# Routing logits with the router's weights stationary: batch 0's in one group ahead of the first scores, G's copy between tile 0's halves, and batch 2's first u block split early

## The chip, the cores and the metric

The kernel runs on one NeuronCore of a Trainium2 chip. Its engines work in parallel and are ordered by semaphores: TensorE (PE; weight loads are listed apart as PEld), VectorE (DVE), ScalarE (ACT), GpSimd (POOL) and the DMA queues, which mostly SyncE (SP) feeds. The metric is the device time of one execution in microseconds, median of several; lower is better.

## The reference

Input x is 4 batches of 1024 rows of 256 floats. Everything is computed from the normalised rows:

```python
xn = layernorm(x)
q, k, v = xn @ Wq.T + bq, xn @ Wk.T + bk, xn @ Wv.T + bv
qk = q @ k.T                                     # per batch, 1024 x 1024
theta = 0.5 + 0.2 * sigmoid(qk) + 0.15 * tanh(qk) + 0.1 * relu(qk)
s = softmax(theta) @ v @ Wo.T + bo
e = argmax(xn @ Wr + br)                         # one of 8 experts per row
g = silu(gelu(xn @ W1[e] + b1[e]) @ W2[e] + b2[e])
out = x + s * g
```

## The kernel before, in words

Most products are split into three float32r matmuls: hi x hi, lo x hi, hi x lo (`product`, L899 to L901). A tile is 128 rows; there are 32 (`NT`), eight per batch (`TPB`). `M` (256 x 256, from Wq and Wk) gives u = M xn; scores are u times xn, so that q and k are never formed. `G` (from Wv and Wo) gives v. A score also needs an offset per row, `c_all` (and `c_half`, half of it), which is one more column of the router's table: `small_w` holds per row of xn 8 expert logits, the offset `E` and zeros up to 48 columns (`PAD`).

Each engine has its program written out by hand; the order in the text is the order in its queue.

- TensorE: transposes batch 0's normalised rows (`turn_0`), makes u of batch 0 (`first_u`, `u_product`), scores of tile 0, `G`, scores of tile 1 with batch 3's transposes between them (`turn`), v of batch 0, then tiles 2 to 7: `scores(n+1)`, `transposes(n)`, `values(n-1)`. Between them it turns batches 3, 2 and 1 (`TURNED`) and computes their logits (`route`). Next come the experts in sorted units of 256 rows (a half unit of 128 where an expert's count ends so), and then tiles 8 to 31 of attention. `job(n)` makes u and v of the next batches in pieces, one per tile: tile 9's and 10's are batch 2's first two blocks of u.
- `route(i, t)` takes tile t of `kept` (transposed rows, fp32) as the stationary operand and streams `small_w` (48 columns) through it, into bank 7; `logits_done` counts batches. `route_0(t)` does that for batch 0 out of `xnT_hi` and `xnT_lo` with `R_parts` (hi and lo of the table) into bank 6: tiles 0 to 3 behind the u products, tiles 4 to 7 between G's four matmuls, with two counts of `logits_done` and of `c_ready`.
- ScalarE: high parts (`high_u`, `high_v`, ...), three activations per half of a tile (`acts`), exponentials (`exps`), gelu; `square_root` for the normalisation.
- VectorE: low parts, `row_statistics`, `variances`, `scales`, the combination of the three activations (`thetas`), `take_turned` (logits and offsets out of bank 7), `finish` (the tile's result out of its bank into `half_0` or `half_s`).
- GpSimd: the normalisation of batches 3, 2 and 1, each waiting for `scales_ready`, later gathers and the last products.

What `turn(i, q)` waits for sets TensorE's pace in the first 60 us: q = 0 for `xn_pool` (GpSimd's normalised rows) and for bank 7 (`G_ready`, later `logits_taken`); q = 1 for bank 6 (`c_ready` for batch 3, `half_s_ready` for batch 1).

## Time and profile before

| what | value |
|---|---|
| time, median of 3 | 527.67 us (527.51 to 527.84) |
| profiled execution's own time | 527.64 us |
| its span, first to last instruction | 525.6 us |
| busy: TensorE, VectorE, ScalarE, GpSimd | 98%, 77%, 66%, 37% |
| granted TensorE clock | 1.000 |

The span is what the trace covers; 2.0 us of the time lie around it. A busy share is an average over the whole; what an edit is worth is read in the stretch where it stands, from what ends the last wait there.

### The profile page before, as it was taken

To read this page: it belongs to the slowest core of one execution; us is meant where nothing else is said; L and a number is where in the kernel's file an instruction comes from. 1 tells how busy PE (TensorE), PEld (TensorE's weight loads), DVE (VectorE), ACT (ScalarE), POOL (GpSimd) and SP (SyncE) were. 2 spreads that over 40 slices of the span, in tenths; PEclk is the share of its full clock that TensorE was granted. 3 is DMA by queue.
4 is the path that set the end of the run, shared out by engine and by line. 5 is a ranking of instruction groups with operands and counts; after the bars stand their busy time and mean duration, and the time that the engine had idled before them with its cause. 6 is when DMAs were issued, how large, how long until landed. Compare 5 with 4: busy or idle time off the path is not lost.

```text
span 525.6 us, 10829 instructions
## 1 busy us (share of the span) xinstructions
PE 515.6 (98%) x3773; PEld 484.3 (92%) x3773; DVE 402.6 (77%) x811; ACT 344.6 (66%) x633; POOL 195.8 (37%) x227
## 2 busy tenths in 40 slices
PE   7999999999999999999999989999999999999997
PEld 6899998899989999899999979998999989999997
DVE  5898689946578855598555688768999998867887
ACT  4789778437356733466343575899787786777884
POOL 3218419913112222222112222005676785342441
PEclk9999999999999999999999999999999999999999
DMA  8964720031635711247311421005233232211221
GB/s 266 344 225 176 285 81 1 2 120 32 230 123 151 255 55 41 61 133 237 112 40 40 136 70 42 21 22 190 62 99 113 71 114 87 62 44 49 60 71 51
DMA packets 40754, 57.49 MB, mean 109 GB/s; under 512 B 3654, under 2 KB 35788, under 8 KB 40156
## 3 DMA queue, kind: packets, MB, share of 16 engines
q1 hardware_dynamic: 35452, 46.02, 26.5%
q0 software_dynamic: 3488, 9.47, 6.4%
q10 hardware_dynamic: 1760, 1.32, 0.8%
q8 instruction: 28, 0.46, 0.4%
q14 instruction: 26, 0.21, 0.1%
HBM read 41.07 MB, written 17.56 MB: 112 GB/s over the span
## 4 chain that ended last, share of the span: by engine, by line
PE 86%; ACT 6%; DVE 5%; issue 1%; POOL 1%; DMA 1%; ACTq 0%; DVEq 0%
PE ps L899 26%; PE ps L901 25%; PE ps L900 25%; PE ps L1014 5%; DVE stats L1375 2%; PE ps L1193 1%; PE ps L1080 1%; ACT hid L763 1%; POOL xn_all L464 1%; DMA xn_all<-in_L_attn_x_dram 1%; PE ps L1070 1%; ACT relu_s L628 1%; ACT tanh_s L625 1%; ACT theta L624 1%; PE ps L1045 1%
## 5 line engine op out<-in xcount | busy, mean ns | idle before, releaser
L899 PE MATMUL ps<-v_hi,pT_hi 128*128 128x258 f32 x256 | 74.9, 293 | 0.2
L747 ACT ACTIVATE hid<-ps,b_now 128x256 f32<-128x256 f32 x128 | 53.7, 472 | 29.7 <-PE ps L901 28.8
L900 PE MATMUL ps<-v_lo,pT_hi 128*128 128x258 f32 x256 | 72.5, 283 | 0.0
L901 PE MATMUL ps<-v_hi,pT_lo 128*128 128x258 f32 x256 | 72.3, 282 | 0.0
L1430 DVE SCALAR_TENSOR_TENSOR theta<-tanh_s,theta 128x512 f32<-128x512 f32 x64 | 47.3, 739 | 23.5 <-ACT tanh_s L625 22.9
L899 PE MATMUL ps<-w_hi_even,hidT_h 128*128 128x256 f32 x200 | 58.5, 293 | 1.6 <-DVE hidT_l L1727 1.1
L636 ACT ACTIVATE theta<-theta,neg_max 128x512 f32<-128x512 f32 x64 | 43.0, 720 | 24.9 <-DVE neg_max L1436 24.6
L519 POOL COPY unit_token<-sorted_token 128x2 int32 x19 | 4.5, 238 | 142.9 <-PE ps L1193 142.9
L901 PE MATMUL ps<-w_hi_even,hidT_l 128*128 128x256 f32 x200 | 56.6, 283 | 0.0
L900 PE MATMUL ps<-w_lo_even,hidT_h 128*128 128x256 f32 x200 | 56.6, 283 | 0.0
L778 ACT ACTIVATE g_sb<-y_sb 128x512 f32<-128x512 f32 x20 | 12.6, 631 | 65.8 <-DVE y_sb L1742 65.8
L624 ACT ACTIVATE theta<-ps,c_half 128x512 f32<-128x512 f32 x64 | 44.3, 692 | 17.4 <-PE ps L901 17.3
L510 POOL DMA_INDIRECT row<-xn_rows,unit_token x38 | 44.1, 1161 | 20.7 <-POOL unit_token L519 14.9
L899 PE MATMUL ps<-xnT_hi,u_hi 128*128 128x512 f32 x128 | 51.7, 404 | 0.0
L526 POOL DMA_INDIRECT g_tile<-sorted_g,slot_g x32 | 37.5, 1171 | 38.0 <-DMA sorted_g<-g_sb 32.7
L901 PE MATMUL ps<-xnT_hi,u_lo 128*128 128x512 f32 x128 | 50.4, 394 | 0.0
L900 PE MATMUL ps<-xnT_lo,u_hi 128*128 128x512 f32 x128 | 50.0, 391 | 0.0
L899 PEld LDWEIGHTS ps<-v_hi,pT_hi 128*128 128x128 f32 x256 | 48.4, 189 | 1.7 <-issue 1.2
L901 PE MATMUL ps<-rowT_h,w_lo_even 128*128 128x256 f32 x176 | 49.8, 283 | 0.0
L899 PE MATMUL ps<-rowT_h,w_hi_even 128*128 128x256 f32 x176 | 49.8, 283 | 0.0
L900 PE MATMUL ps<-rowT_l,w_hi_even 128*128 128x256 f32 x176 | 49.8, 283 | 0.0
L900 PEld LDWEIGHTS ps<-v_lo,pT_hi 128*128 128x128 f32 x256 | 48.6, 190 | 0.3
(258 smaller groups left out, 1641.5 us busy)
## 6 DMA issues: line engine op xcount, KB each, us to landing
w_raw_odd<-in_L_ffn_W_dram SPq DMA_DIRECT2D x10, 1024.0 KB
w_raw_even<-in_L_ffn_W_dram SPq DMA_DIRECT2D x6, 1024.0 KB
sorted_g<-g_sb SPq DMA_DIRECT2D x20, 256.0 KB, 2.2
xn_rows<-xn_all SPq DMA_DIRECT2D x4, 1024.0 KB, 6.2
x_tile<-in_L_attn_x_dram SPq DMA_DIRECT2D x32, 128.0 KB, 2.2
out_dram<-g_tile SPq DMA_DIRECT2D x32, 128.0 KB, 1.7
xn_all<-in_L_attn_x_dram SPq DMA_DIRECT2D x3, 1024.0 KB, 12.4
kept_xT<-passing_xT SPq DMA_DIRECT2D x2, 1024.0 KB, 4.0
```

Of the source, the lines that this page charges most:

```text
L510: pool.indirect_dma_start(row[:, a, :], None, xn_rows, bass.IndirectOffsetOnAxis(ap=tokens[:, a:a + 1], axis=0)).then_inc(row_in, 16)
L526: pool.indirect_dma_start(g_tile[:, p % RING, :], None, sorted_g, bass.IndirectOffsetOnAxis(ap=slot_g[:, n:n + 1], axis=0)).then_inc(g_in[ ...
L624: nc.scalar.activation(theta[:, j % 2, cols], bank, ACT.Tanh, bias=c_half[:, n:n + 1], scale=0.5)
L636: nc.scalar.activation(part, part, ACT.Exp, bias=neg_max[:, j % 2, 1:2], scale=-1.0, accum_out=exp_sums[:, h:h + 1] if n == NT - 1 else No ...
L747: last = nc.scalar.activation(hid[:, j % 2, c * UNIT:(c + 1) * UNIT], ps[:, HID_BANK + j, c * UNIT:(c + 1) * UNIT], ACT.Gelu, bias=b1_now[ ...
L778: nc.scalar.activation(g_sb[:, :, :], y_sb[:, :, :], ACT.Tanh, scale=0.5).then_inc(y_tanh, 1)
L899: mm(dst, a_hi, b_hi, start=first, stop=False)
L900: mm(dst, a_hi, b_lo, start=False, stop=False)
L901: return mm(dst, a_lo, b_hi, start=False, stop=last)
L1014: last = nc.tensor.transpose(pT_bank(n, h)[:, i * P:(i + 1) * P], theta[:, n % 2, h * HALF + i * P:h * HALF + (i + 1) * P], ident[:, :])
L1375: last = v.bn_stats(stats[:, i, :], xn_all[:, i, :])
L1430: v.scalar_tensor_tensor(part, tanh_s[:, cols], KT, part, ALU.mult, ALU.add).then_inc(mixed, 1)
```

## The change

- Router's table stationary. For the group g of 0 to 3, `spread_w` (batches 3, 2, 1) and `R_parts` (batch 0) hold the table's columns at column 32 g of a 128 x 128 operand, zeros elsewhere; the rows that stream through it are those of 32-row group g of all eight tiles, 256 columns in 8 runs of 32. The four groups and two halves of the contraction add up in one 128 x 256 result, and a 32 x 32 block transpose on VectorE brings it into `logits_t`, rows on partitions.
- Batch 0's logits are one block of 16 such matmuls between the u products and tile 0's scores, one count of `logits_done` and `c_ready` for all eight tiles. The other batches' blocks stand whole behind v's last piece and behind `values`.
- ScalarE copies `G_hi` between tile 0's two halves of activations; VectorE puts two tiles of statistics ahead of tile 0's first half and two behind it.
- ScalarE normalises one tile of batch 0 instead of two, VectorE two instead of one, and VectorE's copy of the biases stands ahead of the second statistics.
- In an expert's first unit, `Else` in place of a second `If` (ScalarE, VectorE).
- Batch 2's first block of u is split (`high_u`, `low_u`) at the last expert unit instead of behind tile 10's exponentials; at tile 10 TensorE makes the second block ahead of the tile's transposes.

```diff
+    SPREAD = P + 32
...
-        R_parts = sb("R_parts", [P, DC, PAD], F32R)
+        with ExitStack() as first_routing:
+            R_parts = view(first_routing, "R_parts", [P, DC, 4 * SPREAD], F32R)
...
+        with ExitStack() as routing:
+            spread_w = view(routing, "spread_w", [P, DC, 4 * P])
...
             act.wait_ge(scales_ready, 1)
-            normalize(range(2))
+            normalize(range(1))
...
+            act.wait_ge(key_kept, 1)
+            for g in range(4):
+                nc.scalar.activation(spread_w[:, :, g * SPREAD:g * SPREAD + SM], small_w[:, :, 0:SM], ACT.Copy
+                                     ).then_inc(spread_ready, 1)
             for q in range(2, 4):
                 high_u(0, q)
...
             act.wait_ge(c_ready, 1)
-            for h in range(2):
-                acts(0, h)
+            acts(0, 0)
             act.wait_ge(G_done, 1)
             nc.scalar.activation(G_hi[:, :, :], pair_of(ps[:, 7, :]), ACT.Copy).then_inc(G_high, 1)
+            acts(0, 1)
...
-                with act.If(full < u0 + 1):
+                with act.Else():
...
+            def first_job():
+                high_u(*next_job(TPB + 1)[1:])
+
             with act.If(last_u < full_7):
                 gelus(last_u, 1)
+                first_job()
             with act.If(full_7 < last_u + 1):
-                gelus_half(last_u, 1)
+                gelus_half(last_u, 1, beside=first_job)
...
-                    if job:
+                    if job and n > TPB + 1:
                         (high_u if job[0] == "u" else high_v)(*job[1:])
-                if routed_batch is not None and q % 2:
-                    for t in range(2 * q - 2, 2 * q + 2):
-                        route(routed_batch, t)
+                if routed_batch is not None and q == 3:
+                    route(routed_batch)
...
-                    if routed_batch is not None and i % 4 == 3:
-                        for t in range(i - 3, i + 1):
-                            route(routed_batch, t)
+                    if routed_batch is not None and i == TPB - 1:
+                        route(routed_batch)
...
                     if i == 0:
-                        pe.wait_ge(c_ready, 2)
+                        pe.wait_ge(c_ready, 1)
...
+            def group_of(rows, g):
+
+                return rows.rearrange("p (i g j) -> p g i j", g=4, j=32)[:, g]
+
+            def route(i):
 
                 kept = passing_xT if i < 2 else own_xT
...
+                pe.wait_ge(turned_kept, 4 * i + 4)
+                pe.wait_ge(spread_ready, 4)
+                for g in range(4):
+                    for k in range(DC):
+                        last = mm(ps[:, 7, 0:TPB * 32], spread_w[:, k, g * P:(g + 1) * P], group_of(kept[:, k, :], g),
+                                  start=g == 0 and k == 0, stop=g == 3 and k == DC - 1)
+                last.then_inc(logits_done, 1)
+
+            def route_0():
+
+                pe.wait_ge(R_ready, 1)
+                for g in range(4):
+                    for k in range(DC):
+                        mm(ps[:, 6, 0:TPB * 32], R_parts[:, k, g * P:(g + 1) * P], group_of(xnT_hi[0][:, k, :], g),
+                           start=g == 0 and k == 0, stop=False)
+                        last = mm(ps[:, 6, 0:TPB * 32], R_parts[:, k, g * P:(g + 1) * P], group_of(xnT_lo[0][:, k, :], g),
+                                  start=False, stop=g == 3 and k == DC - 1)
+                last.then_inc(logits_done, 1)
...
-            u_product(0, 2, [0, 1])
-            u_product(0, 3, [2, 3])
+            u_product(0, 2)
+            u_product(0, 3)
+            route_0()
             pe.wait_ge(u_ready, 2)
             scores(0)
...
-                    if m == DC - 1 and ec == DC - 1:
-                        last.then_inc(G_done, 1)
-                    route_0(4 + 2 * m + ec)
+            last.then_inc(G_done, 1)
...
+                elif n == TPB + 2:
+                    job(n)
+                    pe.wait_ge(pT_ready, n * 2)
+                    transposes(n)
+                    weighted(n - 1)
                 else:
+            v.memset(spread_w[:, :, :], 0.0)
+            v.memset(R_parts[:, :, :].bitcast(F32), 0.0)
...
-            normalize(range(2, 3))
-            dve.wait_ge(x0_in[1], 16)
-            statistics = row_statistics(range(4, TPB))
+            normalize(range(1, 3))
             dve.wait_ge(biasT_done, 1)
             v.tensor_copy(bias_cols[:, :], ps[:, 6, BIAS_COL:BIAS_COL + 3 * DC]).then_inc(bias_kept, 1)
-            step(statistics)
+            dve.wait_ge(x0_in[1], 16)
+            step(row_statistics(range(4, TPB)))
...
+            tiles = slice(0, TPB)
             dve.wait_ge(logits_done, 1)
-            score_offsets_0(slice(0, 4))
+            step(v.transpose(logits_t[:, :, :].rearrange("p i n -> p (i n)"), ps[:, 6, 0:TPB * 32]))
+            step(v.tensor_scalar(c_all[:, tiles], logits_t[:, :, E], kappa[:, 0:1], None, ALU.add))
+            step(v.tensor_tensor(c_all[:, tiles], logits_t[:, :, SM + E], c_all[:, tiles], ALU.add))
+            v.tensor_scalar(c_half[:, tiles], c_all[:, tiles], 0.5, None, ALU.mult).then_inc(c_ready, 1)
             scales(2, 3 * TPB, 4 * TPB)
...
             def take_turned(i):
                 b = TURNED[i]
-                dve.wait_ge(logits_done, 3 + i)
+                dve.wait_ge(logits_done, 2 + i)
                 now = slice(b * TPB, (b + 1) * TPB)
-                source = padded(ps[:, 7, 0:TPB * PAD])
-                take_logits(now, source)
-                score_offsets(i, now, source[:, :, E])
-
-            thetas(0, [0])
+                v.transpose(logits_t[:, :, :].rearrange("p i n -> p (i n)"), ps[:, 7, 0:TPB * 32]).then_inc(logits_taken, 1)
+                dve.wait_ge(logits_taken, i + 1)
+                score_offsets(now, logits_t[:, :, E])
+                take_logits(now, logits_t)
...
             dve.wait_ge(x_in[2], 16)
             row_statistics(range(2 * TPB, 2 * TPB + 2))
+            thetas(0, [0])
+            row_statistics(range(2 * TPB + 2, 2 * TPB + 4))
...
-            dve.wait_ge(logits_done, 2)
-            take_logits(slice(0, TPB), logits_0)
+            take_logits(slice(0, TPB), logits_t)
...
-                with dve.If(full < u0 + 1):
+                with dve.Else():
...
-                if next_job(n):
+                if next_job(n) and n > TPB + 1:
...
+            low_u(*next_job(TPB + 1)[1:])
             thetas(TPB + 1)
```

How rows move. The rows below are instructions in program order: line, operation, output <- inputs, output shape; xN is a run. Lines of the change are some 10 higher than those of before (L899 to L901 are L912 to L914).

TensorE of before, batch 0 from u's third block on (`M` is the moving side's partner, `R_parts` the table):

```order
L1111 MATMUL ps<-ident,wo_raw 128x128 x4
L899 MATMUL ps<-xnT_hi,M_hi 128x512
L900 MATMUL ps<-xnT_lo,M_hi 128x512
L901 MATMUL ps<-xnT_hi,M_lo 128x512
L1094 MATMUL ps<-R_parts,xnT_hi 128x48
L1096 MATMUL ps<-R_parts,xnT_lo 128x48
L1094 MATMUL ps<-R_parts,xnT_hi 128x48
L1096 MATMUL ps<-R_parts,xnT_lo 128x48
L899 MATMUL ps<-xnT_hi,M_hi 128x512
```

And of the change, from the end of u's fourth block to tile 0's scores, with the last rows of the block and, behind four products, G:

```order
L914 MATMUL ps<-xnT_hi,M_lo 128x512
L1103 MATMUL ps<-xnT_hi,R_parts 128x256
L1105 MATMUL ps<-xnT_lo,R_parts 128x256
...
L1103 MATMUL ps<-xnT_hi,R_parts 128x256
L1105 MATMUL ps<-xnT_lo,R_parts 128x256
L912 MATMUL ps<-xnT_hi,u_hi 128x512
...
L1132 MATMUL ps<-woT,wv_raw 128x256 x4
L1136 MATMUL ps<-woT,bv_wide 128x256 x2
```

Eight groups of four small matmuls, four between u's products and four between G's, have become one block of 16 wide ones; G's matmuls stand together.

VectorE of before, from the statistics of batch 3 to tile 0's first half:

```order
L1375 BN_STATS stats<-xn_all 128x6 x8
L1382 BN_AGGR mean_var<-stats 128x2 x8
L1384 TENSOR_SCALAR std<-mean_var 128x8
L1533 TENSOR_SCALAR c_all<-ps,kappa 128x4
L1534 TENSOR_TENSOR c_all<-ps,c_all 128x4
L1535 TENSOR_SCALAR c_half<-c_all 128x4
L1389 RECIPROCAL rstd<-std 128x8
L1390 SCALAR_TENSOR_TENSOR shift<-mean_var,rstd 128x8
L1410 SCALAR_TENSOR_TENSOR u_lo<-ps,r_col,u_hi 128x512 x2
L1430 SCALAR_TENSOR_TENSOR theta<-tanh_s,theta 128x512
```

And of the change:

```order
L1396 TENSOR_SCALAR std<-mean_var 128x8
L1545 STREAM_TRANSPOSE logits_t<-ps 128x256
L1546 TENSOR_SCALAR c_all<-logits_t,kappa 128x8
L1547 TENSOR_TENSOR c_all<-logits_t,c_all 128x8
L1548 TENSOR_SCALAR c_half<-c_all 128x8
L1401 RECIPROCAL rstd<-std 128x8
L1402 SCALAR_TENSOR_TENSOR shift<-mean_var,rstd 128x8
L1422 SCALAR_TENSOR_TENSOR u_lo<-ps,r_col,u_hi 128x512 x2
L1387 BN_STATS stats<-xn_all 128x6 x2
L1441 SCALAR_TENSOR_TENSOR theta<-tanh_s,theta 128x512
```

The transpose now stands between `std` and `shift`, and `shift` is what GpSimd's normalisation of batch 3 waits for.

TensorE of before at tile 10 (end of tile 11's scores, tile 10's transposes, u's block, tile 9's values):

```order
L901 MATMUL ps<-xnT_hi,u_lo 128x512
L1014 MATMUL ps<-ident,theta 128x128 x8
L899 MATMUL ps<-xnT_hi,M_hi 128x512
L900 MATMUL ps<-xnT_lo,M_hi 128x512
L901 MATMUL ps<-xnT_hi,M_lo 128x512
...
L899 MATMUL ps<-v_hi,pT_hi 128x258
```

And of the change:

```order
L914 MATMUL ps<-xnT_hi,u_lo 128x512
L912 MATMUL ps<-xnT_hi,M_hi 128x512
L913 MATMUL ps<-xnT_lo,M_hi 128x512
L914 MATMUL ps<-xnT_hi,M_lo 128x512
L912 MATMUL ps<-xnT_hi,M_hi 128x512
L913 MATMUL ps<-xnT_lo,M_hi 128x512
L914 MATMUL ps<-xnT_hi,M_lo 128x512
L1024 MATMUL ps<-ident,theta 128x128 x8
L912 MATMUL ps<-v_hi,pT_hi 128x258
```

u's block has moved from behind the transposes to ahead of them.

## Rows read from the trace of the kernel before

**Rows 1.** The cores' spans and granted TensorE clock; then the page's first part.
```profile
core 0: 525.6 us, clock 1.000
...
PE 515.6 (98%) x3773; PEld 484.3 (92%) x3773; DVE 402.6 (77%) x811; ACT 344.6 (66%) x633; POOL 195.8 (37%) x227
```

**Rows 2.** Timeline of TensorE, 16 to 32 us (start us, us, instruction).
```profile
16.65 0.18 PE L1094 MATMUL ps<-R_parts,xnT_hi 128*128 128x48 f32 x1
...
17.01 0.48 PE L899 MATMUL ps<-xnT_hi,M_hi 128*128 128x512 f32 x1
...
23.30 0.60 PE L1123 MATMUL ps<-woT,wv_raw 128*128 128x256 f32 x2
...
27.49 0.58 PE L899 MATMUL ps<-xnT_hi,u_hi 128*128 128x512 f32 x1
...
28.37 1.39 PE L1070 MATMUL ps<-ident,xn_all 128*128 128x128 f32 x8
...
31.00 1.04 PE L1070 MATMUL ps<-ident,xn_all 128*128 128x128 f32 x8
```

**Rows 3.** What TensorE waited for (us in total, times, longest).
```profile
PE ps L899 <- DVE hidT_l L1727: 1.1, 1, 1.1
...
PE ps L926 <- ACT xn_all L568: 0.3, 1, 0.3
```

**Rows 4.** Timeline of TensorE and ScalarE, 342 to 370 us.
```profile
342.65 1.67 ACT L763 ACTIVATE hid<-ps,b_now 128x128 f32<-128x128 f32 x6 [0.75 <-PE ps L1248]
...
357.98 0.39 PE L899 MATMUL ps<-xnT_hi,u_hi 128*128 128x512 f32 x1
...
359.11 1.09 PE L1014 MATMUL ps<-ident,theta 128*128 128x128 f32 x8 [0.29 <-DVE pT_lo L1451]
...
362.13 0.28 PE L899 MATMUL ps<-v_hi,pT_hi 128*128 128x258 f32 x1
...
367.76 1.03 PE L1014 MATMUL ps<-ident,theta 128*128 128x128 f32 x8
...
370.02 0.28 PE L899 MATMUL ps<-v_hi,pT_hi 128*128 128x258 f32 x1
```

**Rows 5.** Chain of waits at 50 us; timeline of TensorE at 71 us.
```profile
50.15 1.72 PE ps L1080 x16
...
71.15 0.28 PE L1153 MATMUL ps<-running,ones_r 128*128 128x256 f32 x1
71.27 0.17 PE L1154 MATMUL ps<-running,ones_r 128*128 128x8 f32 x1
```

**Rows 6.** Timelines of VectorE, GpSimd, ScalarE and TensorE in the first 12 us.
```profile
1.16 0.28 DVE L1478 MEMSET keep_scan<- 128x264 f32 x1
...
5.33 1.41 DVE L1375 BATCH_NORM_STATS2 stats<-xn_all 128x6 f32<-128x256 f32 x4 [3.60 <-DMA xn_all<-in_L_attn_x_dram]
...
8.03 0.41 DVE L1484 TENSOR_SCALAR xn_all<-xn_all,rstd,shift 128x256 f32<-128x256 f32 x1
...
10.29 0.75 DVE L1490 TENSOR_TENSOR M_lo<-ps,M_hi 128x256 fp32r<-128x256 f32 x2
...
8.11 0.69 POOL L464 TENSOR_SCALAR xn_all<-xn_all,rstd,shift 128x256 f32<-128x256 f32 x1 [3.93 <-DVE shift L1390]
...
10.52 0.58 ACT L657 ACTIVATE xnT_hi<-ps 128x512 fp32r<-128x512 f32 x1
...
10.92 1.17 PE L947 MATMUL ps<-xnT_hi,M_hi 128*128 128x512 f32 x4
```

**Rows 7.** Timeline of GpSimd, 22 to 49 us.
```profile
22.35 5.20 POOL L464 TENSOR_SCALAR xn_all<-xn_all,rstd,shift 128x256 f32<-128x256 f32 x8 [9.83 <-DVE shift L1390]
...
38.60 10.44 POOL L464 TENSOR_SCALAR xn_all<-xn_all,rstd,shift 128x256 f32<-128x256 f32 x16 [10.67 <-DVE shift L1390]
```

**Rows 8.** Timeline of VectorE at 56 us.
```profile
56.06 0.48 DVE L1465 SCALAR_TENSOR_TENSOR half<-ps,rden,attn_const 128x256 f32<-128x256 f32 x1
```

**Rows 9.** Chain of waits at 307 us; ACTq is ScalarE's queue.
```profile
306.93 0.04 ACTq L804
```

More of the change, by code:

```diff
@@ L708, in _ @@
                 high_v(0, q)
-            act.wait_ge(c_ready, 2)
             for n in range(1, TPB):
@@ L839, in tile_8 @@
             def tile_8():
-                act.wait_ge(c_ready, 5)
+                act.wait_ge(c_ready, 4)
                 act.wait_ge(w1_split, 2 * E - 2)
@@ L979, in u_product @@
                         last.then_inc(u_done, 1)
-                    for t in routed[k:k + 1]:
-                        route_0(t)
             def v_product(b, q, routed_batch=None):
@@ L1416, in low_v, with score_offsets @@
                                 v_hi[place_of_batch(b)][:, 2 * q:2 * q + 2, 0:D].bitcast(F32), ALU.subtract).then_inc(v_ready, 1)
-            def score_offsets(i, cols, source):
-                v.tensor_scalar(c_all[:, cols], source, kappa[:, 0:1], None, ALU.add).then_inc(logits_taken, 1)
-                dve.wait_ge(logits_taken, i + 1)
+            def score_offsets(cols, source):
+                step(v.tensor_scalar(c_all[:, cols], source, kappa[:, 0:1], None, ALU.add))
                 v.tensor_scalar(c_half[:, cols], c_all[:, cols], 0.5, None, ALU.mult).then_inc(c_ready, 1)
@@ L1586, in _ @@
                                    ).then_inc(const_kept, 1)
-            row_statistics(range(2 * TPB + 2, 3 * TPB))
+            row_statistics(range(2 * TPB + 4, 3 * TPB))
             dve.wait_ge(x_in[1], 16)
@@ L1760, in first_unit_of @@
                     low_w1(e, other, 0)
-                with dve.If(full < u + 1):
+                with dve.Else():
                     parts_half(u, beside=lambda: low_w1(e, other, 0))
```

45 lines of the change are left out of this document (9 added, 36 removed).

## The prediction

> **What bounds the kernel now.** I read the profile's page and the granted clock first: TensorE is busy 515.6 us of 525.6 us at full clock (1.000 throughout, its 2.4 GHz level), VectorE 77%, ScalarE 66% [rows 1]. So a microsecond taken from TensorE counts only if no wait takes its place, and a stall of TensorE elsewhere is worth as much as work. Then the list of what TensorE waited for, and its timeline around the edits: from 16 to 30 us it runs without a gap [rows 2], the longest waits behind the start are 1.1 us on `hidT_l` and 0.3 us on ScalarE's rows [rows 3], and a stall stands at 359 us [rows 4]. Last the timelines of VectorE and GpSimd beside it: they say when `xn_all`, `G_lo` and `c_all` are ready if TensorE comes earlier. The profiled execution took 527.64 us, the median is 527.67, so I sum against 527.64 and need no correction.
>
> **Batch 0's routing on TensorE.** Before: 32 matmuls of 48 columns. Four of them take 0.36 us from the first to the next product (16.65 to 17.01), and that product's first matmul then runs some 0.09 us slower, so 0.45 us per four, 3.6 us in all [rows 2]. After: 16 of 256 columns. The same kind of instruction (float32r, 256 columns in 8 runs of 32 elements) stands at L1153: the next starts 0.12 us behind it [rows 5]. 16 x 0.12 = 1.9 us. TensorE's own work falls by 1.7 us, 0 to 0.2 us less if the runs cost anything.
>
> **The other three batches' routing.** Before, 16 trace records (8 matmuls) take 1.72 us, 32 of them 3.44 us per batch, and 0.1 us for switching [rows 5]. After, 8 full fp32 matmuls of 256 columns. G's and the constant's are of that size: six of them and 16 small ones take 27.49 - 23.30 = 4.19 us, less 4 x 0.45 is 2.39, so 0.40 each; with the slower matmul behind them 0.44 [rows 2]. 8 x 0.435 = 3.5 us. I book 0, with 0.3 us either way over the two batches where TensorE sets the pace.
>
> **The start.** TensorE waits 0.3 us for ScalarE's two tiles [rows 3]. With one tile on ScalarE and two on VectorE (8.03 + 0.41, some 0.33 more) the last of the four is GpSimd's, 8.11 + 0.69 = 8.80 [rows 6]. That alone gains 0.3 us. But the second tile and the bias copy (which now stands ahead of the statistics) push VectorE's statistics, and with them the square root that stands in ScalarE's queue ahead of the second `xnT_hi` (10.52), by about 0.33 + 0.22 = 0.55 us. That copy would end at 10.52 + 0.58 + 0.55 = 11.65, and the third of the four matmuls of 10.92 needs it at 10.92 + 0.32 + 0.23 = 11.47 [rows 6]. So the 0.3 us turns into a loss of 0.2 to 0.3; I take +0.27 for everything behind it. The two memsets (1024 and 1280 elements; 264 take 0.28, so 1.0 and 1.3 us) fit into the 3.6 us in which VectorE waits for x [rows 6]. The four small copies of `spread_w` stand in ScalarE's idle time before u's third block.
>
> One thing could make the start worse: VectorE's second tile held until GpSimd's ends at 8.80, 0.35 us that the whole chain below would take over. GpSimd's tile beside VectorE's took 0.69 us, against 5.20 / 8 = 0.65 in the long run of them [rows 6, 7], so nothing was held before and I book nothing. The Trainium skill speaks for the hold: its page SBUF — State Buffer, section Who interferes with whom, says that a VectorE tensor_scalar in a two-port mode and GpSimd exclude each other for a whole instruction. By that rule the sum would end 0.35 us higher; this trace, with 0.69 us, doesn't bear it out.
>
> **Where batch 0's 1.7 us go.** TensorE would arrive at batch 3's transposes (28.37 before [rows 2]) at 28.37 - 1.7 + 0.27 = 26.95. They need `xn_all` of batch 3: GpSimd's eight tiles, 22.35 + 5.20 = 27.55 [rows 7]. Those wait for VectorE's `shift`, and ahead of that the change puts the 128x256 transpose out of PSUM. No row has it. Bounds: 0.28 us (a memset of 264 elements, no source at all) and 0.75 us (two `M_lo` operations, 512 elements from PSUM); nearest is one of them, 256 elements, 0.75 / 2 = 0.375 us [rows 6]; I take 0.42 with its wait. So GpSimd ends at 27.55 + 0.27 + 0.42 = 28.24 and TensorE starts there at about 28.3, not at 26.95. `G_lo` is ready before that, about 27.9, although G now waits for one half of tile 0's activations only. Of 1.7 us 1.4 become a new wait on GpSimd. What is gained: the second transpose group no longer waits for `c_ready` 2; these eight took 1.39 us from the first's start to the last's end, the next eight, at 31.00, 1.04 [rows 2]. So TensorE leaves 0.35 + 0.07 = 0.4 us earlier.
>
> **On to batch 2 and 1.** The next group waits for GpSimd's batch 2 (38.60 + 10.44 / 2 = 43.8 [rows 7]). That hangs on tile 1's activations, which follow tile 0's: VectorE's two c_all steps less and two statistics tiles moved ahead bring theta of tile 0 about 0.55 us forward, so 0.6 us here. Batch 1's second group needs `half_0` of tile 0, since it writes the bank that tile's result lies in. Before, it started at 56.6, some 1.7 us behind the routing's end: VectorE did logits, c_all, c_half, then `half` (56.06 + 0.48) [rows 8]. Now all 8 routing matmuls stand at the end and the transpose comes first: 0.42 + 0.2 + 0.2 + 0.3 + 0.2 + 0.5 + 0.1 = 1.9 to 2.0 us. 0.3 us of the 0.6 are lost again. **Front: 0.3 us gained**, between -0.3 (transpose 0.75, VectorE's tile held until 8.80) and +0.7.
>
> **The experts.** `Else` instead of a second `If` drops one compare on ScalarE and VectorE. The only half unit that opens an expert is at 307 us, where TensorE's wait of 1.1 us [rows 3] hangs on ScalarE's queue, in which the compare and its operand's computation stand (0.04 us each, with gaps as long) [rows 9]. 0.1 us.
>
> **Around 359 us.** Tile 11's scores end their last slots 0.69 us (three matmuls of 0.23) behind 357.98, at 358.67; tile 10's transposes start at 359.11, 0.44 late, held by `pT_lo`. From them to the values it takes 362.13 - 359.11 = 3.02 us, for tile 11 370.02 - 367.76 = 2.26 with the same work: 0.76 us more, in which u's product waits for `u_lo` [rows 4]. After: batch 2's first u block is split some 17 us earlier, in a gap in which ScalarE waited 0.75 us for TensorE [rows 4] and VectorE waited too, and the second block's product (six matmuls, 1.4 us) stands ahead of the transposes and covers the 0.44. 0.44 + 0.76 = 1.2 us are gained, 1.15 with something for the early copy. What ScalarE and VectorE no longer do at 359 keeps them ahead of TensorE for the tiles behind; I count half a microsecond of margin left at tile 11's transposes. If ScalarE's early copy (the one of 0.58 us is its like [rows 6]) does not fit the gap whole, it delays tile 9's activations by 0.1. **1.15 us**, 0.5 to 1.3.
>
> **Sum.** 527.64 - 0.3 - 0.1 - 1.15 = 526.1, and the median's 0.03 us more change nothing in it.
>
> **Rivals.**
> - Batch 0's saving arrives in full, because the transposes are not held by GpSimd (the start does not slip, the stall at batch 1 does not grow): 527.64 - 1.7 - 0.1 - 1.15 = 524.7. Against it: GpSimd's 5.2 us start no earlier in any reading.
> - The front gives nothing or costs 0.3 (a transpose of 0.75, or VectorE's second tile held by GpSimd's: 0.35 us turn +0.3 into about 0): 526.4 to 526.8. For it: each step of the front hangs on VectorE's queue.
> - The stall at 359 only moves: the margin of 0.5 us at tile 11 is used up and returns as a wait on `pT_lo`. 527.64 - 0.3 - 0.1 - 0.2 = 527.0.
> - Slower: the fp32 routing matmuls read their 8 runs badly. Sixteen of them stand where TensorE sets the pace; at 0.435 + 1.55 / 16 = 0.53 us each the gain is gone, at 0.60 the kernel is slower by 0.2%, at twice the price 16 x 0.435 = 7.0 us give 533. Against it: L1153 reads such runs at full rate [rows 5], though in the other number format.
>
> **How the numbers follow.** 0.2% (1.06 us, so below 526.6) is about what a measurement can tell here. Forecast (525.5 to 526.5): 0.58; full saving: 0.10; empty front: 0.20, a third of it below 526.6; stall moved: 0.08; slow matmuls: 0.04. Faster 0.58 + 0.10 + 0.07 = 0.75, same 0.20, slower 0.05 (0.04 and what nobody listed). The range 525.0 to 526.9 leaves out most of the full saving, half of the moved stall and the slow matmuls.
>
> **What would show it.** TensorE waits over 1 us on GpSimd's `xn_all` at about 27 us and starts the transposes at 28.2 to 28.4; a transpose of 0.35 to 0.5 us ahead of `shift`; routing blocks of 3.5 us per batch; a wait of 0.6 us on `half` near 56 us; no waits on `pT_lo` and `u_lo` at 359. Wrong if the transposes start near 27, if the start slips by more than 0.5 us, or if a stall stands at tile 11 or 12.

## The result, and the profile after

The changed kernel took 526.48 us (median of 9, 525.39 to 527.29), the kernel before in the same comparison 527.57 us (median of 9, 527.30 to 528.18). The ratio is 0.9977 (95% interval 0.9969 to 0.9986): 1.1 us faster. The predicted time was 526.1 us. Two things beside the medians matter below: the changed kernel's times are spread over 1.9 us and those of the kernel before over 0.9, and the total came out near the forecast although two of its parts did not: the front lost where a gain was booked, and a gain that nobody booked made up for it.

The profiled execution of the changed kernel took 526.14 us with a span of 523.8. This is the page's first part, to be held against [rows 1]:

```profile
core 0: 523.8 us, clock 1.000
...
PE 512.4 (98%) x3709; PEld 480.1 (92%) x3709; DVE 407.2 (78%) x814; ACT 344.7 (66%) x636; POOL 194.4 (37%) x227
```

TensorE has 64 instructions and 3.2 us of busy time less, and yet the span fell by only 1.8 us, because waits came in. They stand in the list of what TensorE waited for (us in total, times, longest), which answers to [rows 3]:

```profile
PE ps L1079 <- POOL xn_all L470: 1.3, 1, 1.3
PE ps L912 <- DVE hidT_l L1737: 1.1, 1, 1.1
PE ps L1079 <- DVE half L1476: 0.8, 1, 0.8
PE ps L939 <- DVE xn_all L1496: 0.7, 1, 0.7
PE ps L1255 <- ACT hid L766: 0.3, 1, 0.3
PE ps L960 <- ACT xnT_hi L663: 0.2, 1, 0.2
```

The first and the third are the waits that the prediction named. The waits on `pT_lo` and `u_lo` at 359 us are gone. The fourth and the last are at the start. A `...` in a view marks rows left out.

TensorE's timeline of the changed kernel shows the front and the stretch at 359 us; it answers to [rows 2] and [rows 4]:

```profile
11.73 0.73 PE L960 MATMUL ps<-xnT_hi,M_hi 128*128 128x512 f32 x2 [0.25 <-ACT xnT_hi L663]
...
16.23 0.48 PE L912 MATMUL ps<-xnT_hi,M_hi 128*128 128x512 f32 x1
...
19.07 0.28 PE L1103 MATMUL ps<-xnT_hi,R_parts 128*128 128x256 f32 x1
...
20.98 0.40 PE L912 MATMUL ps<-xnT_hi,u_hi 128*128 128x512 f32 x1
...
28.48 1.09 PE L1079 MATMUL ps<-ident,xn_all 128*128 128x128 f32 x8 [1.27 <-POOL xn_all L470]
...
39.28 3.61 PE L1094 MATMUL ps<-passing_xT,spread_w 128*128 128x256 f32 x16
42.55 0.58 PE L912 MATMUL ps<-xnT_hi,u_hi 128*128 128x512 f32 x1
...
56.96 0.66 PE L1079 MATMUL ps<-ident,xn_all 128*128 128x128 f32 x4 [0.76 <-DVE half L1476]
...
360.09 1.03 PE L1024 MATMUL ps<-ident,theta 128*128 128x128 f32 x8
...
366.64 1.03 PE L1024 MATMUL ps<-ident,theta 128*128 128x128 f32 x8
```

The same point of the program, by its start in either trace, tells how far the changed kernel is ahead or behind. It is 0.37 us behind at the u product at 16.23 (before: 15.86), 0.11 behind at batch 3's transposes (28.48 against 28.37; most expectations call them tile 3's), 0.13 ahead at 43.7, 0.37 behind at 60, 0.3 behind at 100, 0.16 behind at 298, 0.03 ahead at 308, level at 348, 1.12 ahead at tile 11's transposes (366.64 against 367.76), still 1.1 at 391, and 1.87 ahead at 517. So the gain is made of 0.2 at 308, 1.1 at 359, and two pieces that come in small steps where no instruction was changed: 0.2 between 60 and 298 and 0.75 between 399 and 517. The front loses.

On VectorE, the timeline of the changed kernel, which answers to [rows 6] and [rows 8]:

```profile
2.72 1.12 DVE L1491 MEMSET R_parts<- 128x1280 f32 x1 [0.21 <-issue]
...
8.05 0.91 DVE L1496 TENSOR_SCALAR xn_all<-xn_all,rstd,shift 128x256 f32<-128x256 f32 x2
8.88 0.14 DVE L1512 COPY bias_cols<-ps 128x6 f32<-128x6 f32 x1
8.95 1.39 DVE L1387 BATCH_NORM_STATS2 stats<-xn_all 128x6 f32<-128x256 f32 x4
...
21.70 0.44 DVE L1545 STREAM_TRANSPOSE logits_t<-ps 128x256 f32<-128x256 f32 x1
...
27.51 0.67 DVE L1586 TENSOR_TENSOR G_lo<-ps,G_hi 128x512 fp32r<-128x512 f32 x1
28.10 0.44 DVE L1559 TENSOR_TENSOR logits<-logits_t,br_all 128x64 f32<-128x64 f32 x1
28.57 0.35 DVE L1589 TENSOR_TENSOR logits<-logits,logits_t 128x64 f32<-128x64 f32 x1
28.95 0.69 DVE L1441 SCALAR_TENSOR_TENSOR theta<-tanh_s,theta 128x512 f32<-128x512 f32 x1
...
37.91 0.25 DVE L1401 RECIPROCAL rstd<-std 128x16 f32<-128x16 f32 x1 [0.46 <-ACT std L570]
...
55.46 0.35 DVE L1432 TENSOR_SCALAR c_all<-logits_t,kappa 128x8 f32<-128x8 f32 x1
...
55.92 0.26 DVE L1559 TENSOR_TENSOR logits<-logits_t,br_all 128x64 f32<-128x64 f32 x1
...
56.42 0.48 DVE L1476 SCALAR_TENSOR_TENSOR half<-ps,rden,attn_const 128x256 f32<-128x256 f32 x1
```

Three VectorE rows of before, for the same stretch:

```profile
24.37 0.70 DVE L1430 SCALAR_TENSOR_TENSOR theta<-tanh_s,theta 128x512 f32<-128x512 f32 x1 [0.80 <-ACT tanh_s L625]
...
27.21 0.69 DVE L1574 TENSOR_TENSOR G_lo<-ps,G_hi 128x512 fp32r<-128x512 f32 x1 [0.50 <-ACT G_hi L692]
...
28.97 0.69 DVE L1430 SCALAR_TENSOR_TENSOR theta<-tanh_s,theta 128x512 f32<-128x512 f32 x1
```

And GpSimd of the changed kernel, against [rows 7]:

```profile
23.23 5.20 POOL L470 TENSOR_SCALAR xn_all<-xn_all,rstd,shift 128x256 f32<-128x256 f32 x8 [10.13 <-DVE shift L1402]
```

### The profile page after: what moved, and what is told of

The parts are those of the page before. It is cut to its first block, busy times and chain, and to the rows that moved or that the text cites. A ratio compares the mean times of both kernels' runs of the same rounds, so it can differ in the third digit from the quotient of the medians.

```text
span 523.8 us, 10703 instructions
## 1 busy us (share of the span) xinstructions
PE 512.4 (98%) x3709; PEld 480.1 (92%) x3709; DVE 407.2 (78%) x814; ACT 344.7 (66%) x636; POOL 194.4 (37%) x227
## 4 chain that ended last, share of the span: by engine, by line
PE 89%; DVE 5%; ACT 3%; POOL 1%; issue 1%; DMA 1%; ACTq 0%; DVEq 0%
PE ps L912 27%; PE ps L914 26%; PE ps L913 26%; PE ps L1024 5%; PE ps L1200 1%; PE ps L1094 1%; DVE stats L1387 1%; POOL xn_all L470 1%; DMA xn_all<-in_L_attn_x_dram 1%; ACT hid L772 1%; PE ps L1079 1%; PE ps L1054 1%; DVE u_lo L1422 1%; PE ps L1255 0%; PE ps L960 0%
## 5 line engine op out<-in xcount | busy, mean ns | idle before, releaser
L912 PE MATMUL ps<-v_hi,pT_hi 128*128 128x258 f32 x256 | 74.8, 292 | 0.1
L914 PE MATMUL ps<-v_hi,pT_lo 128*128 128x258 f32 x256 | 72.2, 282 | 0.0
L1441 DVE SCALAR_TENSOR_TENSOR theta<-tanh_s,theta 128x512 f32<-128x512 f32 x64 | 48.4, 756 | 20.1 <-ACT tanh_s L631 19.4
L912 PE MATMUL ps<-w_hi_even,hidT_h 128*128 128x256 f32 x200 | 58.6, 293 | 1.6 <-DVE hidT_l L1737 1.1
L914 PE MATMUL ps<-w_hi_even,hidT_l 128*128 128x256 f32 x200 | 56.5, 283 | 0.0
L912 PE MATMUL ps<-xnT_hi,u_hi 128*128 128x512 f32 x128 | 51.8, 405 | 0.0
L914 PE MATMUL ps<-xnT_hi,u_lo 128*128 128x512 f32 x128 | 50.2, 392 | 0.0
L912 PEld LDWEIGHTS ps<-v_hi,pT_hi 128*128 128x128 f32 x256 | 48.3, 189 | 1.7 <-issue 1.1
L912 PE MATMUL ps<-rowT_h,w_hi_even 128*128 128x256 f32 x176 | 49.8, 283 | 0.0
L914 PE MATMUL ps<-rowT_h,w_lo_even 128*128 128x256 f32 x176 | 49.8, 283 | 0.0
```

The costliest lines, as they stand in the source:

```text
L912: mm(dst, a_hi, b_hi, start=first, stop=False)
L914: return mm(dst, a_lo, b_hi, start=False, stop=last)
L1441: v.scalar_tensor_tensor(part, tanh_s[:, cols], KT, part, ALU.mult, ALU.add).then_inc(mixed, 1)
```

## Experiments

Each kernel was timed beside the kernel before on the same chip; the kernels of one group shared those runs. The kernel before had medians of 527.41, 527.54 and 527.46 us in the three groups. finish_between, start_before, all_three, start_finish and four are medians of 5 executions, the others of 8 to 11.

### First group: the tail, the front, the wait on `half`, the wait on GpSimd

**tail_only**: the kernel before with the edit around 359 us alone.

```diff
+            def first_job():
+                high_u(*next_job(TPB + 1)[1:])
...
+            low_u(*next_job(TPB + 1)[1:])
             thetas(TPB + 1)
...
+                elif n == TPB + 2:
+                    job(n)
+                    pe.wait_ge(pT_ready, n * 2)
+                    transposes(n)
+                    weighted(n - 1)
```

> The kernel before with only the last item of the change: batch 2's first u block split at the last expert unit, and its second block ahead of tile 10's transposes. Theory (the whole gain is the stall at 359 us): 1.1 to 1.2 us faster than before, ratio about 0.9978, and in the trace no wait on pT_lo or u_lo near 359, transposes of tile 11 and later 1.1 us earlier. Rival (the stall only moves, or the gain of the changed kernel comes from the front and from the late tiles' pace): under 0.5 us, ratio 0.999 or more.

Measured: 526.24 us (526.09 to 527.33), ratio 0.9980 (0.9971 to 0.9990), 1.2 us faster. Its trace is 0.16 us behind that of before at 348 us and 0.98 ahead at 375: a gain of 1.14, inside the 1.1 to 1.2 expected. The tail is worth what was booked, without the front.

**front_only**: the changed kernel without the tail's edit and with the second `If` again.

> The changed kernel without its tail edits and with the second If restored: only the first 70 us are changed. Theory (batch 0's saving of 1.7 us becomes a wait on GpSimd, and the block transposes delay the rest): 0.2 to 0.4 us slower than before, ratio 1.0004 to 1.0008, TensorE reaches tile 3's transposes 0.2 to 0.4 us later than before. Rival (the front gains, as the prediction had it): 0.3 us faster, ratio 0.9994.

Measured: 526.99 us (526.54 to 527.79), ratio 0.9992 (0.9983 to 1.0001). By the median that is a gain of 0.4 us and nearer to the rival, but the interval holds 1, so the medians decide nothing. The trace says more. It is of one of the longer executions (527.74 us), 1.04 us behind that of before at batch 3's transposes and 1.07 at 348 us, so up to there the front only costs. Then, from 399 us on, it catches up 0.76 us in the last stage, as the changed kernel did and as tail_only did not. Its first 13 us show where the lag comes from. First VectorE, then TensorE:

```profile
9.84 0.17 DVE L1503 COPY bias_cols<-ps 128x6 f32<-128x6 f32 x1 [1.03 <-PE ps L924]
9.93 1.40 DVE L1378 BATCH_NORM_STATS2 stats<-xn_all 128x6 f32<-128x256 f32 x4
```

```profile
6.50 3.16 PE L919 MATMUL ps<-wk_raw,wq_raw 128*128 128x256 f32 x8
9.59 0.22 PE L924 MATMUL ps<-ident,bias_rows 6*128 6x6 f32 x1
...
17.20 0.48 PE L908 MATMUL ps<-xnT_hi,M_hi 128*128 128x512 f32 x1
```

**finish_between**: the changed kernel, with the reciprocal and `half` of tile 0 between batch 2's transposition and its offsets.

```diff
                 dve.wait_ge(logits_taken, i + 1)
+                if between:
+                    between()
                 score_offsets(now, logits_t[:, :, E])
...
-            take_turned(1)
-            finish(0)
+            take_turned(1, lambda: finish(0))
```

> The changed kernel with tile 0's result (rden and half, 0.65 us) taken on VectorE right behind batch 2's block transpose, ahead of the offsets and the logits. Theory (the 0.76 us wait on half near 56 us is VectorE's order alone): the wait falls to 0.2 or nothing, 0.5 to 0.7 us faster than the changed kernel, so 525.8 to 526.0 us. Rival (another wait stands right behind it, on the turned rows or the exponentials): the wait on half goes and TensorE reaches tile 3's transposes no earlier.

Measured: 525.27 us (524.90 to 525.91), ratio 0.9963 (0.9949 to 0.9977). Its TensorE timeline has the eight transposes in one piece, without the wait:

```profile
55.52 1.29 PE L1079 MATMUL ps<-ident,xn_all 128*128 128x128 f32 x8
```

From there on it is 0.8 us ahead of the changed kernel (0.43 ahead of before at 60 us, where the changed kernel was 0.37 behind). The stall at 56 us was worth 0.8 us by the traces. The median fell by 1.2, more than the 0.5 to 0.7 expected; against padded, a changed kernel of the same group, it is 1.0 lower. No trace shows the rest, and the changed kernel's times alone spread over 1.9 us.

**padded**: the changed kernel with nine needless 256-column matmuls ahead of tile 1's scores.

> The changed kernel with nine needless float32r matmuls of 256 columns (9 x 0.12 = 1.1 us) on TensorE ahead of tile 1's scores. Theory (TensorE waits 1.27 us there for GpSimd's rows): no change of time, the wait on xn_all falls from 1.27 to about 0.2 us. Rival (TensorE's work sets the pace there): 1.1 us slower.

Measured: 526.31 us (525.37 to 526.93), ratio 0.9976 (0.9965 to 0.9986). TensorE's timeline:

```profile
26.84 1.42 PE L1140 MATMUL ps<-M_hi,xnT_hi 128*128 128x256 f32 x9
...
29.12 1.09 PE L1079 MATMUL ps<-ident,xn_all 128*128 128x128 f32 x8 [0.17 <-POOL xn_all L470]
```

The wait on GpSimd went from 1.3 to 0.2 us and the time stayed: 1.1 us of batch 0's saving on TensorE can be spent on nothing and is not missed. This execution, too, had a late start (u product at 16.90), which is why the transposes stand at 29.12.

### Second group: the start, the lie of the tiles, GpSimd's begin

**start_before**: the changed kernel with its first 10 us as before.

```diff
-            normalize(range(1))
+            normalize(range(2))
...
-            normalize(range(1, 3))
+            normalize(range(2, 3))
+            dve.wait_ge(x0_in[1], 16)
+            statistics = row_statistics(range(4, TPB))
             dve.wait_ge(biasT_done, 1)
             v.tensor_copy(bias_cols[:, :], ps[:, 6, BIAS_COL:BIAS_COL + 3 * DC]).then_inc(bias_kept, 1)
-            dve.wait_ge(x0_in[1], 16)
-            step(row_statistics(range(4, TPB)))
+            step(statistics)
```

> The changed kernel with only its start put back: ScalarE normalises tiles 0 and 1, VectorE tile 2, and the copy of the bias columns stands behind the second half's statistics again. In the four profiles at hand whose VectorE copies the bias columns ahead of those statistics, the first u product of batch 0 starts at 16.2, 16.2, 16.9 and 17.2 us, and the bias transposition that the copy waits for ends at 8.4, 8.6, 9.5 and 9.8; in the two profiles with the old order it starts at 15.9 and 16.0, although there the transposition ended at 8.8 and 9.3. Theory (the copy's place passes every late start of TensorE on to the whole front): the u product at 15.8 to 16.1, GpSimd's last normalisation begins near 22.9 and TensorE's transposes of tile 3 near 28.1, the lowest and the highest time are within 1 us of each other (changed kernel: 1.9 us), and the median is 525.7 to 526.0 (changed kernel: 526.48). Rival (the spread and the slip have another cause, the bigger memsets or the group of routing matmuls): u product again at 16.2 or later and a median of 526.3 to 526.6.

Measured: 525.38 us (525.18 to 525.55), ratio 0.9961 (0.9947 to 0.9974). That is 1.1 us less than the changed kernel and more than was expected, and the spread fell from 1.9 to 0.4 us. The bigger memsets and the routing block are still in it, so the rival fell. The edit puts back the tiles of both engines and the place of the copy together; their shares were not tried apart. Its TensorE timeline:

```profile
6.20 1.90 PE L923 MATMUL ps<-wk_raw,wq_raw 128*128 128x256 f32 x8
8.02 0.22 PE L928 MATMUL ps<-ident,bias_rows 6*128 6x6 f32 x1
...
15.83 0.48 PE L912 MATMUL ps<-xnT_hi,M_hi 128*128 128x512 f32 x1
```

Over all traces of this study the pattern holds. With the new start, a bias transposition at 8.14, 8.30, 8.40, 9.22, 9.28 and 9.59 us gave a u product at 16.23, 16.27, 16.18, 16.85, 16.90 and 17.20. With the old one, 8.02, 8.09, 8.40, 8.59, 8.60, 8.64, 9.08 and 9.11 gave 15.83, 15.84, 15.85, 16.01, 15.86, 15.98, 15.91 and 15.95. So the new start costs 0.35 us at best and 1.3 when TensorE's first products are late, and the old one hides the lateness. The spans of all executions say the same, less sharply: they vary by 1.1 to 1.8 us within each of the six kernels with the new start and by 0.3 to 1.1 within those with the old one.

**moved**: the kernel before with one allocation moved and no instruction touched.

```diff
         G_hi, G_lo = sb("G_hi", [P, DC, D], F32R), sb("G_lo", [P, DC, D], F32R)
-        R_parts = sb("R_parts", [P, DC, PAD], F32R)
         small_w = sb("small_w", [P, DC, PAD])
...
         slot_f = sb("slot_f", [P, NT])
+        R_parts = sb("R_parts", [P, DC, PAD], F32R)
```

> The kernel before with one line moved: the 384 bytes per partition of R_parts are allocated behind slot_f and no longer ahead of small_w, so that all tiles between lie 384 bytes lower, as they do in the changed kernel. No instruction is added, removed or moved. In the last stage (399 to 479 us) a tile takes 7.97 us on TensorE in the profiles of the kernel before and of the tail alone, and 7.91 in the four profiles that hold the front edit; over the stage and the six tiles behind it that is 0.6 to 0.8 us. Theory A (where the tiles lie sets that pace): 7.91 us a tile and a median of 526.6 to 526.9. Theory B (something else of the front edit sets it, or chance): 7.97 us a tile and a median of 527.2 to 527.6.

Measured: 526.66 us (526.27 to 527.84), ratio 0.9982 (0.9973 to 0.9991): 0.9 us faster with the same program. Theory A. Two tiles of the last stage, tile starts on TensorE, ten tiles apart; first the kernel before, then this one:

```profile
431.19 1.04 PE L1014 MATMUL ps<-ident,theta 128*128 128x128 f32 x8
...
505.23 1.04 PE L1014 MATMUL ps<-ident,theta 128*128 128x128 f32 x8
```

```profile
430.99 1.03 PE L1014 MATMUL ps<-ident,theta 128*128 128x128 f32 x8
...
504.49 1.04 PE L1014 MATMUL ps<-ident,theta 128*128 128x128 f32 x8
```

74.04 us became 73.50. At 298 us the moved kernel is 0.18 ahead, at 517 us 0.82. In the last tiles, which hold no product of u or v, the scores take 2.74 us a tile instead of 2.77 and the products of `v` and `pT` 2.97 instead of 2.99, while the eight transposes take 0.79 in both. Earlier in the stage the products that make u and v, 1.50 us a tile, do not change either. So what the old place costs sits in the scores and in the products of `v` and `pT`.

**scales_first**: the changed kernel with batch 3's scales ahead of the transposition.

> The changed kernel with batch 3's scales and shifts (0.4 us) ahead of the transposition of batch 0's logits and no longer behind the offsets. GpSimd's eight normalisations, which began at 23.2 us, then begin at 22.3 to 22.5 and end at 27.5 to 27.7, with TensorE at its transposes of tile 3 by 27.3. Theory (TensorE's wait of 1.3 us is that late begin): the wait falls to 0.2 to 0.5 us and the median to 525.5 to 525.9. Rival (theta of tile 0, 0.92 us twice on VectorE, is the next to be late): the wait falls but TensorE waits for theta or pT of tile 0 near 31.5, and the median is 526.1 to 526.4.

Measured: 526.17 us (525.46 to 527.20), ratio 0.9973 (0.9964 to 0.9982), 0.3 us below the changed kernel and within its spread. My theory fell; the median lies in the rival's range, but TensorE waited neither for theta nor for `pT`. The wait did not shrink, it changed its name. In the list of TensorE's waits:

```profile
PE ps L1079 <- DVE G_lo L1586: 1.5, 1, 1.5
```

The transposes write the bank in which G lies, and VectorE must have computed `G_lo` from it first. In the changed kernel's trace `G_lo` ended at 28.18 and GpSimd at 28.43 us: both conditions were met within 0.3 us of each other, and taking one away shows the other.

**all_three**: start_before, finish_between and scales_first together.

> The changed kernel with the start of the kernel before, with batch 3's scales ahead of the transposition, and with the first steps of batch 0's finish between batch 2's transposition and its offsets. If the three gains add (0.5, 0.8 and 1.0 us by the two expectations beside this one and by the measured 525.27 for the third), the median is 524.2 to 524.6. If scales first and the start hide each other (both move GpSimd's begin, and TensorE then has no more wait there), it is 524.6 to 525.0.

Measured: 524.72 us (524.57 to 525.34), ratio 0.9953 (0.9939 to 0.9966), above the sum of three gains and in the second range: scales first added nothing.

### Third group: the lie of the tiles again, and the best version

**moved_back**: the changed kernel with 384 unused bytes ahead of `small_w`.

```diff
+        unused = sb("unused", [P, DC, PAD], F32R)
         small_w = sb("small_w", [P, DC, PAD])
```

> The changed kernel with 384 bytes per partition that nothing uses allocated ahead of small_w, so that small_w and the tiles behind it up to slot_f lie again where they lie in the kernel before. No instruction is changed. If where the tiles lie is worth the 0.9 us that the kernel before gained by the move, this kernel loses as much: tiles at 7.97 us in the last stage and a median of 527.1 to 527.5, level with the kernel before. If the changed kernel does not react to it: 7.91 us a tile and a median of 526.3 to 526.7.

Measured: 526.66 us (525.68 to 527.57), ratio 0.9985 (0.9976 to 0.9994). The expected loss of 0.7 us does not show in the median, which is 0.2 above that of the changed kernel; both have the spread of the late start, so the medians can't decide. The traces do. The changed kernel's two tiles, then this one's:

```profile
429.94 1.03 PE L1024 MATMUL ps<-ident,theta 128*128 128x128 f32 x8
...
503.45 1.03 PE L1024 MATMUL ps<-ident,theta 128*128 128x128 f32 x8
```

```profile
430.47 1.04 PE L1025 MATMUL ps<-ident,theta 128*128 128x128 f32 x8
...
504.51 1.04 PE L1025 MATMUL ps<-ident,theta 128*128 128x128 f32 x8
```

73.51 us became 74.04, the kernel before's figure to the hundredth. The place of the tiles costs this trace what was expected; the median shows a loss of 0.2 us (0.4 by the ratios, whose intervals overlap) of the 0.7 expected, and that gap stays open.

**moved_half**: the kernel before with the tiles 192 bytes lower instead of 384.

> The kernel before with its tiles 192 bytes lower instead of 384 (R_parts moved as before, and 192 unused bytes in its place). If the pace falls in step with the distance, or depends on lying at a multiple of 384, the median is between the two, 526.9 to 527.2, or that of the kernel before; if a shift of 192 does what one of 384 does, it is 526.5 to 526.8. I know no reason for one above the other.

Measured: 526.63 us (526.30 to 527.14), ratio 0.9984 (0.9975 to 0.9993), the gain of the full shift. Its two tiles:

```profile
431.08 1.04 PE L1015 MATMUL ps<-ident,theta 128*128 128x128 f32 x8
...
504.48 1.04 PE L1015 MATMUL ps<-ident,theta 128*128 128x128 f32 x8
```

73.40 us. The distance is not what counts; the old place was a bad one among three.

**start_finish**: start_before and finish_between together.

> The changed kernel with the start of the kernel before and with the first steps of batch 0's finish between batch 2's transposition and its offsets, without scales first. The start alone gave 525.38 us; the wait for half is 0.8 us in its profile. Theory (the two gains are apart in time and add): 524.5 to 524.7, with no wait for half near 56 us; then the batch 3 scales of the kernel with all three (524.72) gave nothing. Rival: 524.9 to 525.4.

Measured: 524.63 us (524.38 to 525.57), ratio 0.9945 (0.9931 to 0.9958), the lowest median of the study, 1.9 us below the changed one and 2.8 below the kernel before. It has no wait on `half`, and all_three is level with it, so batch 3's scales gave nothing.

**four**: all_three with `G_lo` two statistics earlier.

```diff
-            row_statistics(range(2 * TPB + 2, 2 * TPB + 4))
             dve.wait_ge(G_high, 1)
             v.tensor_tensor(G_lo[:, :, :], pair_of(ps[:, 7, :]), G_hi[:, :, :].bitcast(F32), ALU.subtract
                             ).then_inc(G_ready, 1)
+            row_statistics(range(2 * TPB + 2, 2 * TPB + 4))
```

> The kernel with all three edits, and G_lo's subtraction on VectorE ahead of the two row statistics (0.7 us) that stood before it. In that kernel TensorE's transposes of tile 3 waited 1.5 us and began at 28.3, right behind G_lo's end (28.2), while GpSimd had been done since 27.35. Theory (with GpSimd early, G_lo is what the transposes wait for): they begin at 27.5 to 27.7, the wait is 0.7 to 0.9 us, and the median is 523.9 to 524.2. Rival (theta of tile 0 on VectorE is as late as ever and takes the gain back at tile 0's transposes near 31.5): TensorE waits there and the median is 524.5 to 524.8.

Measured: 524.96 us (524.61 to 525.13), ratio 0.9951 (0.9938 to 0.9965), above both ranges. The transposes started at 27.84, 0.5 us earlier than in all_three, with a wait of 0.85. Eight microseconds later the gain was lost. In its TensorE timeline:

```profile
27.84 1.06 PE L1079 MATMUL ps<-ident,xn_all 128*128 128x128 f32 x8 [0.85 <-DVE G_lo L1588]
...
36.22 0.39 PE L912 MATMUL ps<-G_hi,xnT_hi 128*128 128x256 f32 x1 [0.63 <-ACT relu_s L634]
```

The rival was right in kind and wrong in place: not theta near 31.5 on VectorE, but v's product at 36.2, which waits until ScalarE's `relu_s` has read its scores. VectorE's theta of tile 0's second half came no earlier than in all_three (28.87 against 28.69, after a start 0.17 later), as the rival had it, and ScalarE's exponentials and tile 1's activations follow it. After GpSimd and VectorE, ScalarE is the third engine that holds this stretch.

## Why the prediction came out right, step by step

The total was within 0.4 us of the measured one, and the sign was right. Two terms of it were not, and they cancelled: that the sum came out is luck. The clock that it read as 1.000 throughout was at its lower level for the first 5.8 to 9.1 us, which differs from one execution to the next, and the change made the front wait for it.

- **Around 359 us, 1.15 us gained:** right. 1.14 in the trace of tail_only, 1.12 in that of the changed kernel (0.00 at 348 us, 1.12 ahead at 366.64), and no stall at tile 11 or 12.
- **The experts, 0.1 us gained:** right in mechanism, 0.19 in the trace (0.16 behind at 298 us, 0.03 ahead at 308; front_only, which keeps the second `If`, gains nothing there). Up to that point front_only differs from the changed kernel in the second `If` alone, so the 0.19 us are `Else`'s; the rest of the change was not needed for it (start_before and finish_between gain 0.19 there too).
- **Batch 0's routing:** right. The sixteen matmuls took 0.12 us each (19.07 to 20.98, 1.91 us). TensorE arrived at 27.2, waited 1.27 us for GpSimd and began at 28.48 (booked 28.3), and padded shows that 1.1 of the 1.7 us are unused. The transposition took 0.44 us (booked 0.42). The 0.4 us by which TensorE was to leave earlier were 0.2 (29.33 against 29.52).
- **The other batches' routing, 0:** the block in fp32 took 3.27 us from its first matmul to the next product (39.28 to 42.55), plus 0.1 us for the slower matmul behind it, 0.1 less than the 3.5 worked out.
- **Front, "0.3 us gained": this step failed.** It lost 0.37 us in the profiled execution (at 60 us) and 1.0 to 1.2 us in those of padded, scales_first and front_only. Three parts of it were mis-sized. First, the start: booked 0.27 us, measured 0.3 to 1.3 at the u product, and over the 0.5 us that the prediction named as a sign of being wrong in three of the six traces. The working counted for VectorE's copy only the time that it takes, 0.22 us, as if TensorE's bias transposition always were done by then. The copy is a wait on TensorE, and its place ahead of the statistics puts the whole chain of the front behind an event that moves by 1.6 us between executions (8.02 to 9.59 us), with the moment at which the clock rises. Second, the 0.6 us forward for tile 1: theta of tile 0's second half began at 28.95, where it had begun at 28.97. Before, VectorE had waited 0.80 us for ScalarE ahead of the first theta and 0.50 ahead of `G_lo`; now it has no idle time from 23 to 31 us, begins that stretch later, and three of its operations beside GpSimd took longer (0.92 for 0.70 at the first theta, 0.44 and 0.35 for 0.27 and 0.28 at the logits, one input of which now lies in SBUF and no longer in PSUM). VectorE's own steps for tile 1 did come forward by the booked amount, its theta to 36.03 from 36.70, but it then waited 0.46 us for ScalarE's square root, which stands behind tile 1's activations and ran at 37.68 against 37.69. So GpSimd's batch 2 began at 38.48 instead of 38.60: the path went through ScalarE, and the working had it on VectorE. Third, the stall at batch 1: booked as 0.3 lost of 0.6 gained, measured as 0.6 us lost of 0.24 gained (55.00 against 55.24 just ahead of it, 57.37 against 57.01 behind). With finish_between it vanishes.
- **Not booked: where the tiles lie, 0.75 us gained in the last stage and up to 0.2 ahead of it.** The change also moved `R_parts` out of its old place, and everything behind it up to `slot_f` came to lie 384 bytes lower. The moved kernel has this alone, with 0.9 us by the medians and 0.82 in the trace. Only tile starts, mostly between 399 and 517 us, show it; in the list of waits it doesn't exist.

Added up for the profiled execution: 0.37 lost at the front, 0.2 gained slowly between 60 and 298 us (the moved kernel gains 0.16 there), 0.19 at 308, 1.1 at 359, 0.75 in the last stage, 1.87 in all, which is the difference at 517 us.

Of the rivals, the full saving fell (the transposes are held), the stall at 359 did not move, and the fp32 matmuls read their runs at full rate. "The front gives nothing or costs 0.3" was the true one, with a larger cost, and its time of 526.4 to 526.8 holds the measured median; my forecast's 525.5 to 526.5 holds it too. Without the shift of the tiles the traces make 0.8 us more of it, near 527.3 and outside the predicted range; the median of moved_back, 526.66, doesn't bear that out, and the spread of the starts is too wide for it to decide.

On the hold of VectorE's second tile: GpSimd's own took 0.69 us again, and VectorE's two took 0.91 us together, where 0.41 and 0.33 were booked: 0.17 us, not 0.35. The Trainium skill's rule of an exclusive lock for the whole instruction (SBUF — State Buffer, Who interferes with whom) would give the full 0.35; this row lies halfway, and no row shows whether the operation ran in a two-port mode, for which alone the rule is stated.

What stays open: which of the moved tiles makes the last stage slow in its old place, and by what mechanism. No experiment moved a single one. Open as well is a tile near 415 us that took from 7.91 to 8.33 us over the 14 traces, in the longest of them with a wait for `xnT_lo`; it adds up to 0.4 us to an execution, and nothing was tried on it.

## What to carry to other kernels

Before a copy or a wait is put ahead of a long chain on an engine, ask how far the event it waits for moves from one execution to the next; one trace gives one value, and the spread over executions hints at the rest (spans 1.1 to 1.8 us apart with the copy ahead, 0.3 to 1.1 with it behind). When a change also moves a buffer, time the kernel before with the buffer moved and nothing else: here that one line gave 0.9 us, against 1.1 for the whole change. Where engines reach a point within half a microsecond of each other, expect little from an edit to one of them: here scales_first gained nothing in TensorE's wait, and the 0.5 us that four gained were taken back 8 us later.

## What the runs showed of the hardware

- The same instructions ran at two paces, by where the tiles lie in SBUF: 74.04 us for ten tiles in the three traces with the old place (before, tail_only, moved_back), 73.40 to 73.51 in the eleven with a new one, a difference of 0.7% with TensorE busy throughout. From 399 to 517 us, without the tile at 415, it is 109.71 us in all three and 108.91 in ten of the eleven (moved_half: 108.71). Shifts of 192 and of 384 bytes did nearly the same.
- TensorE's first four fp32 products (eight rows) took 1.89 to 3.16 us with the same inputs and a start at 6.2 to 6.5 us. Their rows start 0.43 us apart up to some moment and 0.22 behind it. The record of the granted clock begins, at 1.00, between 5.8 and 9.1 us in the 14 traces, and behind 7 us in all in which the four products took over 2.1 us. The Trainium skill (TensorE: Matmul & The Clock Gate, Part 1) says that the engine starts at its lower level and that the moment at which it rises varies from run to run, and these traces agree.
- VectorE's operations with two inputs in SBUF were slower while GpSimd was normalising. In the changed kernel the custom max step of theta took 0.93 us beside it and 0.69 alone in its first form, 0.93 and 0.75 in its second. The Trainium skill states such a contention for two SBUF inputs (SBUF — State Buffer, Who interferes with whom), and the trace agrees for that step; the theta step itself took 0.70 to 0.92 us beside GpSimd over the traces and 0.69 alone, so the size is not fixed.
- A VectorE transposition of 128x256 float32 out of PSUM took 0.44 us. A memset of 264 float32 elements took 0.28 us, of 1024 0.91 us and of 1280 1.12 us, which is 0.8 ns for one more element.
